# Decoder block on one core: the first batch of x in four transfers, its moments and transposes tile by tile, 14 warming products for 26

## The chip, the core and the metric

The kernel runs on one core of a Trainium2 chip. A core has a matrix engine (TensorE, here PE, with its weight loads listed apart as PEld), a vector engine (VectorE, DVE), a scalar engine (ScalarE, ACT), a general engine (GpSimd, POOL), a queue-only engine (SyncE, SP) and 16 DMA engines that move data between HBM and SBUF. Each engine runs its own stream of instructions in program order; the streams meet only in semaphores that one engine raises and another waits on. Matrix products read SBUF and write PSUM banks; DVE and ACT read PSUM and write SBUF. The metric is the device time of one execution in microseconds.

## The reference

```python
x = x + attn(layernorm(x), q_weight, v_weight, out_w, out_b)     # x is (4, 512, 256)
x = x + xattn(layernorm(x), ctx, ...)                            # 16 heads of 64, 64 keys a batch
x = x + ffn(layernorm(x), Ws, bs, W1, b1, W2, b2)                # 8 experts, each takes its top 256 rows

def attn(x, q_weight, v_weight, out_w, out_b):                   # attention over the first axis, of length 4
    q = einsum('tbm,mhd->tbhd', x, q_weight)
    q_sq = einsum('tbhd,tbhd->tbh', q, q)
    squared_dist = q_sq[:, None] + q_sq[None, :] - 2.0 * einsum('tbhd,sbhd->tsbh', q, q)
    attn_weights = softmax(-squared_dist / sqrt(head_dim), axis=1)
    A = einsum('mhd,nhd->hmn', q_weight, q_weight) / sqrt(head_dim)
    PXA = einsum('tsbh,sbhm->tbhm', attn_weights, einsum('tbm,hmn->tbhn', x, A))
    return einsum('tbhm,mhd->tbhd', PXA, v_weight).reshape(...) @ out_w.T + out_b
```

All of it is computed in float32. Only the first few microseconds of the first line matter for this change.

## The kernel before, in words

The program is written as one stream per engine (`sp_part1`, `act_part1`, `dve_part1`, `pool_part1`, `pe_part1`, and parts 2 to 4 behind them). Nothing is reordered by a planner: what stands in a function is the order on that engine, and the only thing that makes an engine wait is a semaphore.

x has 4 x 512 rows of 256, held in SBUF as `X`, 16 tiles of 128 rows; tile `t * NJ + j` holds rows 128j to 128j + 127 of position t. The first attention mixes the four positions t of one row, so part 1 works in four blocks j of T = 4 tiles each. "The first batch" is block j = 0.

The way of block 0 to the first use of its queries, with the semaphores in brackets:

- SP starts all loads, in the order x block 0, `wqa` (the query weight), x block 1, ctx, two more weights, x blocks 2 and 3, and then the four 1 MB weights Wq, Wk, Wv, Wo. The load of one x block is one transfer of 512 KB [`ld_x[j]`].
- DVE, `statistics(0)`: four BN_STATS (one a tile), then four BN_AGGR, which give mean and variance of each row [`var1_ready`].
- POOL, `inverse_std`: adds eps, raises to -0.5 [`powers`, after two of its four operations], then multiplies the mean by it and negates it [`rstd1_ready`].
- The four normalised tiles `xn1` are made by two engines: tiles 1 to 3 by DVE (line 673, behind `powers`), tile 0 by ACT (`normalise(0, (0,))`, behind `rstd1_ready`). Each raises `xn1_ready` by one.
- PE, `xn_transpose(0)`: eight 128 x 128 transposes (four tiles, two column halves m) into banks 0 and 1, behind `xn1_ready` = 4.
- ACT, `xnT_evac(0)`: copies both banks to `xnT` [`xnT_ready`].
- PE, `q_product(0)`: eight float32 products of 128 x 256 [`full`], after four transposes of ctx.
- ACT copies the queries to `q` [`q_ready`], and DVE's `differences(0)` (lines 643 to 645) forms the differences of the positions' queries. From there the chain goes on to squares (ACT), distances and weights (DVE), and so through the block.

Ahead of its first transpose PE runs `WARM_UP` = 26 products of the identity with itself, whose result nothing reads. They wait for the identity alone.

DVE's order around this matters for the prediction: `statistics(0)`, the three normalised tiles, `statistics(1)`, `statistics(2)`, `statistics(3)`, each behind its block's load, and only then `differences(0)`. So does the order on PE: warming, transposes of block 0, ctx transposes (behind the load of ctx), `q_product(0)`.

Of the kernel before, what the change touches and what calls it, by code (L numbers as in the profile page):

```python
# [13 lines left out]
def build_program(nc, A, out):  # L14
# [108 lines left out]
    with ctx:  # L123
# [6 lines left out]
        def overlay(*sets):  # L130
# [96 lines left out]

        ld_x = [sem(f"ld_x{j}") for j in range(NJ)]
        ld = {n: sem(f"ld_{n}") for n in ("cols", "ctx", "wqa", "attw", "outb", "small", "ws", "wq", "wk", "wv")}
        xn3_stored = sem("xn3_stored")  # L230
# [11 lines left out]
        H_hi_ready, H_ready = sem("H_hi_ready"), sem("H_ready")  # L242
        var1_ready, rstd1_ready, xn1_ready, xnT_ready, q_ready = (
            sem(n) for n in ("var1_ready", "rstd1_ready", "xn1_ready", "xnT_ready", "q_ready"))
        dif_ready, sq_ready, dist_ready, ex_ready, weighted, summed, scaled, mixed, mixT_ready = (
# [88 lines left out]
        def sp_part1(sp):  # L334
            def load_x(j):
                sp.dma_start(X[:, j::NJ, :], x_rows[:, j::NJ, :]).then_inc(ld_x[j], 16)

            load_x(0)
            sp.dma_start(wqa[:], wq_s).then_inc(ld["wqa"], 16)
            load_x(1)  # L340
            sp.dma_start(ctx_sb, ctx_rows).then_inc(ld["ctx"], 16)
            sp.dma_start(owa, ow_s).then_inc(ld["attw"], 16)
            sp.dma_start(wva, wv_s).then_inc(ld["attw"], 16)
            load_x(2)
            load_x(3)
            sp.dma_start(Wq[:], chunked(A["L0_xattn_Wq"])).then_inc(ld["wq"], 16)
            sp.dma_start(Wk[:], chunked(A["L0_xattn_Wk"])).then_inc(ld["wk"], 16)
            sp.dma_start(Wv[:], chunked(A["L0_xattn_Wv"])).then_inc(ld["wv"], 16)
            sp.dma_start(Wo[:], chunked(A["L0_xattn_Wo"])).then_inc(xn3_stored, 16)
# [47 lines left out]
        def pool_part1(pool, order):  # L397
# [19 lines left out]
            for s in range(NJ):  # L417
                if s >= 1:
                    pool.wait_ge(scaled, s)
                    g.tensor_tensor(acc[:], acc[:], q[:, (s - 1) % 2], ALU.add).then_inc(mixed, 1)  # L420
                pool.wait_ge(xn1_ready, T * (s + 1))
                g.tensor_tensor(X[:, s::NJ, :], X[:, s::NJ, :],
                                outb_bc[:].unsqueeze(1).to_broadcast([P, T, D]), ALU.add).then_inc(xb_ready, 1)
# [19 lines left out]
        def act_part1(act):  # L443
            a = nc.scalar
            def normalise(j, tiles=range(T)):
# [3 lines left out]
                for t in tiles:  # L449
                    i = t * NJ + j  # L450
                    a.activation(xn1[:, t], X[:, i], ACT.Identity, bias=nmean[:, i:i + 1],
                                 scale=rstd[:, i:i + 1]).then_inc(xn1_ready, 1)

# [66 lines left out]
            act.dma_start(bs_bc[:], row_broadcast(A["L0_ffn_bs"], E)).then_inc(ld["small"], 16)  # L520
            act.wait_ge(ld_x[0], 16)
            xnT_evac(0)
# [64 lines left out]
        def dve_part1(dve, order):  # L587
            v = nc.vector

            def statistics(j, var_ready):  # L590
                for t in range(T):
                    ins = v.bn_stats(stats[:, t * NJ + j, :], X[:, t * NJ + j, :])
                order(ins)
# [73 lines left out]

            dve.wait_ge(ld_x[0], 16)
            statistics(0, var1_ready)
            dve.wait_ge(powers, 1)  # L670
            for t in range(1, T):
                i = t * NJ
                v.tensor_scalar(xn1[:, t], X[:, i], mv[:, i, 0:1], rstd[:, i:i + 1], ALU.subtract,
                                ALU.mult).then_inc(xn1_ready, 1)
            for j in range(1, NJ):
# [51 lines left out]

        WARM_UP = 26

        def pe_part1(pe):  # L730
            t = nc.tensor

            def xn_transpose(j):
# [67 lines left out]
            for _ in range(WARM_UP):  # L801
                t.matmul(banks[7][:, 0:P], ident[:], ident[:], start=True, stop=True)  # L802
            xn_transpose(0)
            pe.wait_ge(ld["ctx"], 16)
# [1197 lines left out]
```

## Time and profile before

| | |
|---|---|
| runs | 354.67, 352.87, 354.94 us; median 354.67 us |
| profiled execution | 353.8 us, its span in the trace 351.9 us, mean granted TensorE clock 0.952 |
| PE busy | 312.6 us (89% of the span) |
| DVE busy | 289.1 us (82%) |
| POOL busy | 198.7 us (56%) |
| ACT busy | 188.6 us (54%) |
| moved by DMA | 34.26 MB |

The profile is of one execution. Times in it count from the start of the span. A row of the timeline or of the chain of waits begins with its start and its length in us; the chain of waits is the work that ended last, followed back from the end of the kernel, so that an operation in it delayed what followed. A float32 product on PE stands in the trace as two records.

### The profile page before, as it was taken

What the parts mean: (1) busy time and instruction counts of PE and PEld (TensorE: products, weight loads), DVE (VectorE), ACT (ScalarE), POOL (GpSimd) and SP (SyncE); (2) the same over time, 40 slices, a digit from 0 to 9 for tenths busy, and PEclk for the clock granted to TensorE, in tenths of its full rate; (3) what the DMA queues carried; (4) which work ended last, traced back from release to release, by engine and by line L of the source; (5) the groups of instructions that cost most, each with busy time, mean ns of one, the idle gap of its engine ahead of it and who ended that gap; (6) DMA issues with size and microseconds to landing.
All of it is one profiled execution on the core that took longest, in us unless ns stands there. A gap on an engine that the chain in (4) does not pass through costs nothing.

```text
span 351.9 us, 6208 instructions
## 1 busy us (share of the span) xinstructions
PE 312.6 (89%) x2200; PEld 277.3 (79%) x2200; DVE 289.1 (82%) x664; ACT 188.6 (54%) x374; POOL 198.7 (56%) x256
## 2 busy tenths in 40 slices
PE   7988999998789999999999992129999999999991
PEld 7877787776579999999999891128999998899990
DVE  2789899979988988788887877778798997999960
ACT  1576765448536565667655645790426736742230
POOL 3768898853234458877888765703264623643232
PEclk9999999999999999999999995556999999999998
DMA  8970000000000406225042437301367957621222
GB/s 244 378 251 1 3 0 2 0 2 1 0 2 15 136 16 210 71 81 182 30 149 77 134 106 241 119 1 32 95 200 191 262 154 207 151 28 32 32 30 30
DMA packets 24045, 34.26 MB, mean 97 GB/s; under 512 B 1784, under 2 KB 20560, under 8 KB 23888
## 3 DMA queue, kind: packets, MB, share of 16 engines
q1 hardware_dynamic: 20112, 29.36, 25.6%
q0 software_dynamic: 3072, 4.20, 7.0%
q10 hardware_dynamic: 832, 0.32, 0.4%
q8 instruction: 17, 0.28, 0.3%
q14 instruction: 12, 0.10, 0.1%
HBM read 27.58 MB, written 6.29 MB: 96 GB/s over the span
## 4 chain that ended last, share of the span: by engine, by line
PE 65%; DVE 19%; POOL 6%; issue 3%; DMA 3%; ACT 2%; POOLq 0%; DVEq 0%; ACTq 0%
PE bank L970 9%; PE bank L972 8%; PE bank L971 8%; PE bank L1742 5%; PE bank L1010 4%; PE q_banks L970 4%; PE q_banks L972 3%; PE q_banks L971 3%; PE bank L802 3%; PE bank L1743 2%; DVE flags_all L1485 2%; DMA out_x<-ybuf,idx 2%; PE q_banks L747 2%; PE bank L765 2%; PE bank L781 2%
## 5 line engine op out<-in xcount | busy, mean ns | idle before, releaser
L1816 POOL DMA_INDIRECT out_x<-ybuf,idx x16 | 26.2, 1637 | 46.9 <-DVE ybuf L1840 44.7
L1742 PE MATMUL bank<-W,h_hi 128*128 128x512 f32 x112 | 41.0, 407 | 0.2
L970 PE MATMUL bank<-H,PT_hi 128*128 128x256 f32 x128 | 36.5, 285 | 0.4 <-DVE PT_lo L1293 0.3
L1161 ACT ACTIVATE prob<-prob 128x1024 f32<-128x1024 f32 x16 | 17.0, 1060 | 36.2 <-DVE prob L1335 36.2
L972 PE MATMUL bank<-H,PT_lo 128*128 128x256 f32 x128 | 36.2, 283 | 0.0
L971 PE MATMUL bank<-H,PT_hi 128*128 128x256 f32 x128 | 36.2, 283 | 0.0
L1201 POOL TENSOR_TENSOR prob<-prob,rsum 128x1024 f32<-128x1024 f32 x15 | 28.6, 1906 | 12.1 <-DVE rsum L1310 12.1
L1795 POOL DMA_INDIRECT xg<-xn_rows,idx x16 | 20.6, 1285 | 26.0 <-DVE idx L1873 22.0
L1772 ACT ACTIVATE hbuf<-bank,b_cols 128x256 f32<-128x256 f32 x32 | 13.5, 472 | 37.1 <-PE bank L972 37.1
L1743 PE MATMUL bank<-W,h_lo 128*128 128x256 f32 x112 | 31.4, 280 | 0.0
L970 PEld LDWEIGHTS bank<-H,PT_hi 128*128 128x128 f32 x128 | 24.5, 191 | 1.5 <-issue 0.9
L1742 PEld LDWEIGHTS bank<-W,h_hi 128*128 128x128 f32 x112 | 21.1, 188 | 5.6 <-DVE h_lo L1929 1.2
L971 PEld LDWEIGHTS bank<-H,PT_hi 128*128 128x128 f32 x128 | 24.5, 191 | 0.5
L972 PEld LDWEIGHTS bank<-H,PT_lo 128*128 128x128 f32 x128 | 24.5, 191 | 0.0
L1929 DVE TENSOR_TENSOR h_lo<-hbuf,h_hi 128x512 fp32r<-128x512 f32 x32 | 22.2, 693 | 1.1
L1743 PEld LDWEIGHTS bank<-W,h_lo 128*128 128x128 f32 x112 | 21.2, 189 | 0.0
L1293 DVE TENSOR_TENSOR PT_lo<-bank,PT_hi 128x512 fp32r<-128x512 f32 x32 | 20.0, 666 | 1.1 <-ACT PT_hi L1125 1.1
L1304 DVE TENSOR_REDUCE sums<-prob 128x16 f32<-128x1024 f32 x15 | 18.3, 1220 | 2.8 <-ACT prob L1161 2.4
L1772 ACT ACTIVATE hbuf<-q_banks,b_cols 128x256 f32<-128x256 f32 x32 | 13.4, 471 | 11.9 <-PE q_banks L972 6.0
L1010 PE MATMUL bank<-ident,prob 128*128 128x128 f32 x128 | 17.1, 276 | 2.8 <-DVE H L947 2.8
L1927 DVE CAST h_hi<-hbuf 128x512 fp32r<-128x512 f32 x32 | 14.2, 445 | 5.6 <-ACT hbuf L1772 5.6
L1186 POOL TENSOR_TENSOR rstd<-mv,eps_col 128x1 f32<-128x1 f32 x16 | 3.1, 192 | 27.9 <-DVE mv L1312 24.9
(298 smaller groups left out, 1088.6 us busy)
## 6 DMA issues: line engine op xcount, KB each, us to landing
W_raw<-in_L_ffn_W SPq DMA_DIRECT2D x8, 1024.0 KB, 5.6
W_in<-in_L_ffn_W SPq DMA_DIRECT2D x8, 1024.0 KB, 6.5
X<-in_x SPq DMA_DIRECT2D x4, 512.0 KB, 6.4
xn_rows<-xn SPq DMA_DIRECT2D x16, 128.0 KB, 1.7
out_x<-X SPq DMA_DIRECT2D x4, 512.0 KB, 3.6
Wq<-in_L_xattn_Wq SPq DMA_DIRECT2D x1, 1024.0 KB, 11.0
Wk<-in_L_xattn_Wk SPq DMA_DIRECT2D x1, 1024.0 KB, 12.3
Wv<-in_L_xattn_Wv SPq DMA_DIRECT2D x1, 1024.0 KB, 15.1
```

The lines of the kernel that those rows point to most:

```text
L970: t.matmul(out_ps, hi, rhs_hi, start=first, stop=False)
L971: t.matmul(out_ps, hi, rhs_lo, start=False, stop=False)
L972: return t.matmul(out_ps, lo, rhs_hi, start=False, stop=last_one)
L1010: mm = t.transpose(banks[4 + g][:, c * P:(c + 1) * P], flat[:, o:o + P], ident[:])
L1201: g.tensor_tensor(prob[:, s], prob[:, s], rsum[:, s].unsqueeze(2).to_broadcast([P, HX, CK]), ALU.mult).then_inc(prob_ready, 1)
L1293: nc.vector.tensor_tensor(PT_lo[:, n % 2, c], v3(banks[4 + g][:], 4), raw(PT_hi[:, n % 2, c]), ALU.subtract).then_inc(PT_ready, 1)
L1742: t.matmul(v3(banks[6 + h][:], 2), h_hi[:, f, hs], W2[:, f, :, p], start=f == 0, stop=False)
L1743: mm = t.matmul(banks[6 + h][:, 0:D], h_lo[:, f, hs], W2_hi[:, p, f], start=False, stop=f == FC - 1)
L1772: ins = a.activation(hbuf[:, g % 2, f % 2], banks[g][:, (f % 2) * CAP:(f % 2 + 1) * CAP], ACT.Gelu_apprx_tanh, bias=b1_cols[:, e * FC + f: ...
L1795: g.indirect_dma_start(xg[:, s, h], None, xn3_dram, bass.IndirectOffsetOnAxis(ap=idx[:, e, h:h + 1], axis=0), bounds_check=last_row, oob_i ...
L1816: g.indirect_dma_start(out_flat, bass.IndirectOffsetOnAxis(ap=idx[:, e, h:h + 1], axis=0), ybuf[:, h], None, bounds_check=last_row, oob_is ...
L1929: v.tensor_tensor(h_lo[:, fs], hbuf[:, g_ % 2], raw(h_hi[:, fs]), ALU.subtract).then_inc(h_ready, 1)
```

## The change

- The load of x block 0 becomes four transfers of 128 KB, one a tile, each with a semaphore of its own (`ld_x0[t]`). They stand where the one transfer stood, first on SP. Blocks 1 to 3 are loaded as before.
- DVE's `statistics(0)` waits for each tile just ahead of that tile's BN_STATS; the wait for the whole block in front of it is gone.
- DVE's three normalised tiles now raise `first_xn1_ready`, one each. ACT's tile 0 raises `xn1_ready` by T = 4 at once, so that all later counts of `xn1_ready` stay as they were. POOL, which writes over X block 0 later (line 422), waits for both.
- PE's eight transposes of block 0 (`first_xn_transposes`) go tile by tile, in the order 1, 2, 3, 0, each pair behind its own tile. Before, all eight waited for all four tiles, and went bank by bank.
- `WARM_UP` is 14.

```diff
@@ sp_part1
-            load_x(0)
+            for t in range(T):
+                sp.dma_start(X[:, t * NJ, :], x_rows[:, t * NJ, :]).then_inc(ld_x0[t], 16)
             sp.dma_start(wqa[:], wq_s).then_inc(ld["wqa"], 16)
@@ pool_part1
                 pool.wait_ge(xn1_ready, T * (s + 1))
+                if s == 0:
+                    pool.wait_ge(first_xn1_ready, T - 1)
@@ act_part1, normalise
                     a.activation(xn1[:, t], X[:, i], ACT.Identity, bias=nmean[:, i:i + 1],
-                                 scale=rstd[:, i:i + 1]).then_inc(xn1_ready, 1)
+                                 scale=rstd[:, i:i + 1]).then_inc(xn1_ready, T if j == 0 else 1)
@@ act_part1
-            act.wait_ge(ld_x[0], 16)
+            for t in range(T):
+                act.wait_ge(ld_x0[t], 16)
             xnT_evac(0)
@@ dve_part1, statistics
                 for t in range(T):
+                    if j == 0 and var_ready is var1_ready:
+                        dve.wait_ge(ld_x0[t], 16)
                     ins = v.bn_stats(stats[:, t * NJ + j, :], X[:, t * NJ + j, :])
@@ dve_part1
-            dve.wait_ge(ld_x[0], 16)
             statistics(0, var1_ready)
             dve.wait_ge(powers, 1)
             for t in range(1, T):
                 i = t * NJ
                 v.tensor_scalar(xn1[:, t], X[:, i], mv[:, i, 0:1], rstd[:, i:i + 1], ALU.subtract,
-                                ALU.mult).then_inc(xn1_ready, 1)
+                                ALU.mult).then_inc(first_xn1_ready, 1)
@@ pe_part1
-        WARM_UP = 26
+        WARM_UP = 14
...
+            def first_xn_transposes():
+
+                ps = [bank_free(f"T0{m}") for m in range(MC)]
+                for r in (*range(1, T), 0):
+                    pe.wait_ge(*((first_xn1_ready, r) if r else (xn1_ready, T)))
+                    for m in range(MC):
+                        mm = t.transpose(ps[m][:, r * P:(r + 1) * P], xn1[:, r, m * P:(m + 1) * P], ident[:])
+                        if r == 0:
+                            filled(mm, f"T0{m}")
...
-            xn_transpose(0)
+            first_xn_transposes()
             pe.wait_ge(ld["ctx"], 16)
```

On PE, from its first product to the first query product, the stream before reads as follows (line, operation, output and inputs, and in brackets what it waits for; `xn` is xn1, `dif` at line 809 the buffer in which ctx lies):

```order
L802 MATMUL bank<-ident 128x128 [waits ident_ready]
L802 MATMUL bank<-ident 128x128 x25
L738 MATMUL bank<-ident,xn 128x128 [waits xn1_ready]
L738 MATMUL bank<-ident,xn 128x128 x7
L809 MATMUL bank<-ident,dif 128x128 [waits ld_ctx]
L809 MATMUL bank<-ident,dif 128x128 x3
L747 MATMUL q_banks<-wqa,xnT 128x256 [waits xnT_ready,ld_wqa]
```

and now:

```order
L818 MATMUL bank<-ident 128x128 [waits ident_ready]
L818 MATMUL bank<-ident 128x128 x13
L745 MATMUL bank<-ident,xn 128x128 [waits first_xn1_ready]
L745 MATMUL bank<-ident,xn 128x128
...
L745 MATMUL bank<-ident,xn 128x128 [waits xn1_ready]
L745 MATMUL bank<-ident,xn 128x128
L825 MATMUL bank<-ident,dif 128x128 [waits ld_ctx]
L825 MATMUL bank<-ident,dif 128x128 x3
L763 MATMUL q_banks<-wqa,xnT 128x256 [waits xnT_ready,ld_wqa]
```

Twelve warming products are gone, one wait became four, and what comes behind the transposes kept its place.

On SP, the loads of part 1 before:

```order
L336 DMA X<-in_x 128x4x256
L339 DMA wqa<-in_L_attn_q_weight 128x2x256
L336 DMA X<-in_x 128x4x256
L341 DMA dif<-in_ctx 128x2x256
L342 DMA dif<-in_L_attn_out_w 128x2x256
L343 DMA dif<-in_L_attn_v_weight 128x2x256
L336 DMA X<-in_x 128x4x256 x2
```

and now:

```order
L340 DMA X<-in_x 128x256 x4
L341 DMA wqa<-in_L_attn_q_weight 128x2x256
L337 DMA X<-in_x 128x4x256
L343 DMA dif<-in_ctx 128x2x256
L344 DMA dif<-in_L_attn_out_w 128x2x256
L345 DMA dif<-in_L_attn_v_weight 128x2x256
L337 DMA X<-in_x 128x4x256 x2
```

Every later load, x block 2 among them (the first of the pair in the last row), now stands three issues further back.

On DVE, from the first moments to the moments of block 2 before:

```order
L592 BN_STATS stats<-X 128x6 [waits ld_x0]
L592 BN_STATS stats<-X 128x6 x3
L595 BN_AGGR mv<-stats 128x2 [waits dve_order]
L595 BN_AGGR mv<-stats 128x2 x3
L673 TENSOR_SCALAR xn<-X,mv,rstd 128x256 [waits powers]
L673 TENSOR_SCALAR xn<-X,mv,rstd 128x256 x2
L592 BN_STATS stats<-X 128x6 [waits ld_x1]
...
L592 BN_STATS stats<-X 128x6 [waits ld_x2]
```

and now:

```order
L599 BN_STATS stats<-X 128x6 [waits ld_x0_0]
L599 BN_STATS stats<-X 128x6 [waits ld_x0_1]
L599 BN_STATS stats<-X 128x6 [waits ld_x0_2]
L599 BN_STATS stats<-X 128x6 [waits ld_x0_3]
L602 BN_AGGR mv<-stats 128x2 [waits dve_order]
L602 BN_AGGR mv<-stats 128x2 x3
L679 TENSOR_SCALAR xn<-X,mv,rstd 128x256 [waits powers]
L679 TENSOR_SCALAR xn<-X,mv,rstd 128x256 x2
L599 BN_STATS stats<-X 128x6 [waits ld_x1]
...
L599 BN_STATS stats<-X 128x6 [waits ld_x2]
```

The order of the work is the same; the one wait in front of the four BN_STATS is now one wait ahead of each, and the wait for x block 2 is where it was.

## Rows read from the trace of the kernel before

**Rows 1.** Chain of waits, first 17 us: start, length, engine, tile, line.

```profile
1.83 8.86 PE bank L802 x52
10.69 0.45 PE bank L738 x4
11.23 1.09 ACT xnT L457 x2
12.46 3.71 PE q_banks L747 x16
16.19 0.61 ACT q L464
```

**Rows 2.** Timeline of DVE to 17 us; in brackets idle time before, and its releaser.

```profile
4.83 1.41 DVE L592 BATCH_NORM_STATS2 stats<-X 128x6 f32<-128x256 f32 x4 [4.83 <-DMA X<-in_x]
6.27 0.38 DVE L595 BATCH_NORM_AGGREGATE mv<-stats 128x2 f32<-128x6 f32 x4
8.19 1.32 DVE L673 TENSOR_SCALAR xn<-X,mv,rstd 128x256 f32<-128x256 f32 x3 [1.54 <-POOL rstd L406]
...
10.85 0.38 DVE L595 BATCH_NORM_AGGREGATE mv<-stats 128x2 f32<-128x6 f32 x4
11.58 1.41 DVE L592 BATCH_NORM_STATS2 stats<-X 128x6 f32<-128x256 f32 x4 [0.35 <-DMA X<-in_x]
...
13.31 1.37 DVE L592 BATCH_NORM_STATS2 stats<-X 128x6 f32<-128x256 f32 x4
...
16.82 0.96 DVE L643 TENSOR_TENSOR dif<-q_banks,q 128x768 f32<-128x768 f32 x1 [1.72 <-ACT q L464]
```

**Rows 3.** Warming products still to come from two times on: ns min/median/max, first and last start.

```profile
L802 PE MATMUL bank<-ident x46: 274/275/421, 3.3 to 10.4; 128*128 128x128 f32 x46 
...
L802 PE MATMUL bank<-ident x25: 274/275/275, 7.7 to 10.4; 128*128 128x128 f32 x25 
```

**Rows 4.** Window: PE, PEld, DVE, ACT, POOL busy, granted clock, DMA share, GB/s.

```profile
3.00:4.00 1.00, 1.00 (x7) 1.00 (x6) 0.00 (x0) 0.00 (x0) 0.00 (x0) 1.00 1.04 348
```

**Rows 5.** Timeline of the SP queue; last, all issues of 128 KB stores (ns).

```profile
0.79 0.42 SPq L336 DMA_DIRECT2D X<-in_x  x1
...
1.82 0.46 SPq L336 DMA_DIRECT2D X<-in_x  x1
2.32 0.51 SPq L341 DMA_DIRECT2D dif<-in_ctx  x1
...
3.92 1.06 SPq L336 DMA_DIRECT2D X<-in_x  x2
...
7.69 0.71 SPq L348 DMA_DIRECT2D Wv<-in_L_xattn_Wv  x1
...
L1407 SPq DMA_DIRECT2D xn_rows<-xn x16: 319/332/343, 110.4 to 218.3; - x16
```

**Rows 6.** Issue to landing in us: x blocks 0, 1, ctx, x block 2, Wv; last, later stores.

```profile
X<-in_x SPq DMA_DIRECT2D x1, 512.0 KB, 4.0
...
X<-in_x SPq DMA_DIRECT2D x1, 512.0 KB, 5.2
dif<-in_ctx SPq DMA_DIRECT2D x1, 256.0 KB, 5.8
...
X<-in_x SPq DMA_DIRECT2D x1, 512.0 KB, 7.6
...
Wv<-in_L_xattn_Wv SPq DMA_DIRECT2D x1, 1024.0 KB, 15.1
...
xn_rows<-xn SPq DMA_DIRECT2D x16, 128.0 KB, 1.7
```

**Rows 7.** Timeline of ACT, PE and POOL further on.

```profile
8.82 0.60 ACT L451 ACTIVATE xn<-X,nmean,rstd 128x256 f32<-128x256 f32 x1 [6.53 <-POOL nmean L408]
...
26.10 1.28 POOL L438 TENSOR_TENSOR acc<-dif 128x512 f32<-128x512 f32 x1 [2.18 <-DVE dif L664]
...
27.99 1.03 PE L781 MATMUL bank<-ctxT,Wv 128*128 128x256 f32 x4
```

More of the change, by code:

```diff
@@ L228, in build_program @@
         ld_x = [sem(f"ld_x{j}") for j in range(NJ)]
+        ld_x0 = [sem(f"ld_x0_{t}") for t in range(T)]
         ld = {n: sem(f"ld_{n}") for n in ("cols", "ctx", "wqa", "attw", "outb", "small", "ws", "wq", "wk", "wv")}
@@ L242, in build_program @@
         H_hi_ready, H_ready = sem("H_hi_ready"), sem("H_ready")
-        var1_ready, rstd1_ready, xn1_ready, xnT_ready, q_ready = (
-            sem(n) for n in ("var1_ready", "rstd1_ready", "xn1_ready", "xnT_ready", "q_ready"))
+        var1_ready, rstd1_ready, xn1_ready, first_xn1_ready, xnT_ready, q_ready = (
+            sem(n) for n in ("var1_ready", "rstd1_ready", "xn1_ready", "first_xn1_ready", "xnT_ready", "q_ready"))
         dif_ready, sq_ready, dist_ready, ex_ready, weighted, summed, scaled, mixed, mixT_ready = (
```

## The prediction

> **What bounds the kernel now.** I read the chain of waits first, for what stands in the first microseconds, since every edit lies there. It shows PE alone from 1.83 us on: the 26 warming products, then the transposes, then the copy on ACT, the query products, the copy of the queries, and behind them DVE's differences [rows 1, 2]. The reader is to see that the chain's first 9 us are products whose result nobody reads. The four normalised tiles were ready earlier: DVE's three at 8.19 + 1.32 = 9.51 us [rows 2], ACT's one at 8.82 + 0.60 = 9.42 us [rows 7]. The last warming record starts at 10.4 us and lasts 0.275 us [rows 3]. So the transposes waited about a microsecond for the warming, and below that, hidden by it, lies the chain load, moments, POOL, normalised tiles.
>
> Next the DVE timeline, for what comes when both get shorter. DVE goes from block 0's tiles to the moments of blocks 1, 2 and 3, and only then to `differences(0)`. It already waits in there, 0.35 us for x block 2 until 11.58 us, and it ends at 16.82 - 1.72 = 15.10 us, 1.72 us ahead of the queries [rows 2]. Those 1.72 us are the room for every gain at the start: past them DVE, and through it the load of x block 2, sets the time. The landings confirm it: block 2 was issued at 3.92 us and took 7.6 us, so it landed at 11.52 us [rows 5, 6].
>
> **The change part by part.**
>
> *The moments.* The 512 KB landed at 0.79 + 4.0 = 4.79 us [rows 5, 6], and then came four BN_STATS in 1.41 us and four BN_AGGR, to 6.65 us [rows 2]. With a tile each, three of the BN_STATS run while later tiles land, and only the last stands behind the last landing: 1.41 / 4 = 0.35 us in place of 1.41, a gain of 1.06 us if the last tile lands at 4.79 us as the block did. No row shows a load split so. The bounds: the last tile could land earlier or later by what the issue moves. The fourth issue starts later by three issues, 3 x 0.33 to 3 x 0.42 us, 1.0 to 1.3 us (the 128 KB stores' issue, and that of the whole block [rows 5]). Of that little should reach the landing: from 3 us on the DMA engines are busy without a break, at 348 GB/s [rows 4], and the 512 KB need 1.5 us at that rate, so the fourth tile's bytes come last either way. I take 4.8 us, and keep 4.5 to 5.4. So `var1_ready` comes at 5.6 instead of 6.65 us.
>
> *The normalised tiles.* POOL's way is the same work: DVE starts 1.54 us after the moments, ACT 2.17 us after [rows 2, 7]. Tiles 1 to 3 then run from 7.14 to 8.46 us, the first done at 7.6; ACT's tile is ready at 8.37 us. Signalling tile by tile costs nothing that a row shows, since each of these instructions raised a semaphore before too.
>
> *The warming products.* 46 of the 52 records were left at 3.3 us and 25 at 7.7 us, so 21 records took 4.4 us, 0.21 us each; the last 24 steps took 2.7 us, 0.11 us each [rows 3]. That is the lower and the upper of the clock's two levels (1.2 and 2.4 GHz) by the spacing, though the column of the granted clock reads 1.00 from 3 to 4 us, in the slow stretch [rows 4]; I go by the spacing. PE had run products without a break since 1.83 us when the rate doubled, about 7.5 us. Fourteen products are 28 records; the 28th started at 7.7 us and ended at about 8.0 us. So 12 products, 2.7 us, are gone, and the end of the warming now falls at 8.0 us, 0.4 us behind the first tile and ahead of the last. The warming no longer decides.
>
> *The transposes.* Tiles 1 and 2 follow the warming at once, tile 3 at 8.46 us, tile 0 at about 8.7 us: four records of 0.11 us behind the last tile, and the first full bank at about 8.95 us. Before, four transposes ended at 11.14 us and ACT began at 11.23 us [rows 1]; now it begins near 9.0 us. Both banks are filled by the last pair, so ACT can no longer copy bank 0 while bank 1 is filled; that costs about two records, 0.2 us, and is in the sum. ACT's copies take 1.09 us and the first query product begins at 12.46 - 11.23 = 1.23 us behind them [rows 1], at 10.2 us. The ctx transposes ahead of it need ctx, which landed at 2.32 + 5.8 = 8.1 us [rows 5, 6] and now between that and 9.4 us (by the 1.3 us above); their four records fit before 10.2 us either way. The query products end at 13.9 us, ACT's last copy at 14.5 us, against 16.80 [rows 1]. This branch gains 2.3 us.
>
> *What is late next.* DVE ends block 0's tiles at 8.46 us and block 1's moments 1.72 us later (9.51 to 11.23 us before [rows 2]), at 10.2 us; block 1 landed at 7.02 us [rows 5, 6], and even 1.3 us later it is there. Then DVE waits for x block 2. Its bytes stand behind all that SP issued before it, and the engines are saturated, so a later issue should be made good in the queue: between 0 and 1.3 us of delay, and I take 0.2, near zero, since the row nearest to it is the DMA share above 1.0 [rows 4]. From 11.52 + 0.2 = 11.7 us, two blocks of moments (11.58 to 15.10 us before, 3.52 us [rows 2]) end at 15.25 us. The queries are there at 14.5 us. So `differences(0)` starts at 15.3 instead of 16.82 us: a gain of **1.5 us**, of 2.3 that PE's branch offers.
>
> *Behind that* I see nothing that gives it back. POOL, busy with tables until then, waits 2.18 us for DVE's weighted differences at 26.10 us [rows 7]; its own work moves up by about 1 us with the moments. The last load that part 1 waits for, Wv, landed at 7.69 + 15.1 = 22.8 us and is first used beside Wk at 27 us [rows 5 to 7]; 1.5 us earlier on one side and up to 1.3 later on the other still leave room. From there on every wait is on another engine, so the shift goes through to the end.
>
> *The sum.* The profiled execution took 353.8 us, 0.9 under the median of the three runs, 354.67. These four times average 354.07 us, and I set the sum on that: 354.07 - 1.5 = **352.6 us**.
>
> **The rivals.**
>
> *The queue delay reaches x block 2.* All 1.0 to 1.3 us of the three issues arrive, DVE's moments end at 16.2 to 16.4 us, and the gain is 0.4 to 0.6 us: 353.6 us. For it: DVE waited there already. Against it: engines that never run dry.
>
> *The whole of PE's branch counts.* If block 2 lands 0.8 us earlier, as its issue gets ahead of the small loads of ACT's queue or because the transfers settle faster, 2.3 us arrive: 351.8 us. Against it: nothing in the change brings it forward.
>
> *The query products run at the lower clock* (slower). The rate doubled at record 26 or 27, and the change keeps 28. If in an execution it doubles later, or the pauses between the four pairs put it off, the query products, 3.71 us [rows 1], take 7.4: from 10.2 to 17.6 us, the copy to 18.2 us, and `differences(0)` starts 1.4 us later than before, 355.5 us. It decides once the products are slow for more than about 2.3 of their 3.71 us. Against it: while the clock is low the transposes too take twice as long and fill PE's pauses. The Trainium skill, "TensorE: Matmul & The Clock Gate", Part 1, says that how many products run slowly at the start differs from run to run of one kernel and should not be fitted to a count; by it, a fixed 14 is a margin of one product here that another execution may not have. One trace cannot show the spread.
>
> *The transfers land one after the other* (slower). A 128 KB transfer on a quieter queue takes 1.7 us from issue to landing [rows 6]. If each of the four had to land before the next moves on, the last tile would come at 0.79 + 4 x 1.7 = 7.6 us, 2.8 us later than the block did, and x block 2 behind it at 14.3 us; two blocks of moments then end at 17.9 us, and `differences(0)` starts 1.0 us later than before: 355.1 us. It decides once block 2 lands over 1.7 us late. Against it: x block 1 landed 2.2 us and ctx 3.3 us after block 0 although each took over 5 us from its issue [rows 5, 6], so transfers of one queue overlap. The Trainium skill, "DMA: Bandwidth & Descriptors", Anatomy of one DMA, gives a fixed cost of some 2 us to each transfer and its rules advise large ones; paid in series, three more would cost 6 us, and the landings just named disagree with that.
>
> **How the numbers follow.** The forecast has 0.62, the queue delay 0.15, the whole branch 0.10, the lower clock 0.08, the serial landing 0.05. Predicted is 352.6 us. The range goes from 351.2 (the fastest run, 352.87, less the whole room of 1.7) to 355.0 us, which leaves out most of the lower clock and a little of the noise, since the four times of one kernel spread over 2.1 us. A change of 1% (3.5 us), about what a measurement of this kernel can tell from none, is more than any branch gives: faster by over 1% has 0.05 (the whole branch with a lucky median), slower by over 1% 0.03 (the lower clock for longer than the query products), within 1% 0.92.
>
> **What would show it.** In the profile after, the warming ends near 8 us or earlier; block 0's BN_STATS are spread between 4 and 5.2 us; DVE's moments end near 5.6 us; `xnT` begins near 9 us and the query products near 10.2 us, in 3.7 us; DVE waits more than 1 us for x block 2, and `differences(0)` follows the moments of block 3 without a wait, near 15.3 us. A DVE wait for ACT's `q` there would say that PE's branch decides after all; query products of over 5 us, the clock; a later part of the chain that starts at the old times, that something behind took the gain back.

## The result and the profile after

The changed kernel took 356.81 us (median of 9 runs, 356.07 to 360.00), the kernel before 354.03 us (9 runs, 352.53 to 354.94), timed in turn: a ratio of **1.0095** (95% interval 1.0071 to 1.0118). It is slower by 2.8 us where 352.6 us was predicted, outside the range and in the other direction. The profiled execution of after is its slowest, 360.0 us with a span of 358.0. Runs over 1.5% above the fastest of their kernel are left out of the ratios but not of the medians, so the two can differ, and the profile of outb_late below is of such a run and is not read.

The chain of waits of after (start, length, engine, tile, line) no longer begins with the warming:

```profile
5.51 9.16 DMA X<-in_x
14.70 1.42 DVE stats L599 x4
16.52 1.38 DVE stats L599 x4
20.11 1.48 ACT sq L474
21.59 0.98 ACT xnT L461 x2
22.62 5.42 PE q_banks L763 x16
...
61.23 1.09 PE bank L772 x8
```

It starts with one load, x block 2. The DVE timeline of after, in answer to [rows 2]:

```profile
2.98 0.43 DVE L599 BATCH_NORM_STATS2 stats<-X 128x6 f32<-128x256 f32 x1 [2.98 <-DMA X<-in_x]
3.63 0.86 DVE L599 BATCH_NORM_STATS2 stats<-X 128x6 f32<-128x256 f32 x2 [0.22 <-DMA X<-in_x]
5.53 0.43 DVE L599 BATCH_NORM_STATS2 stats<-X 128x6 f32<-128x256 f32 x1 [1.04 <-DMA X<-in_x]
...
14.70 1.41 DVE L599 BATCH_NORM_STATS2 stats<-X 128x6 f32<-128x256 f32 x4 [3.76 <-DMA X<-in_x]
...
18.22 0.93 DVE L650 TENSOR_TENSOR dif<-q_banks,q 128x768 f32<-128x768 f32 x1
```

The tiles' moments are spread over their landings, as foreseen, and DVE waits 3.76 us for x block 2, with no wait between block 3's moments and `differences(0)`, as foreseen too. But block 2 comes at 14.70 us, not at 11.7, against 11.58 before. Of those 3.12 us of delay the 1.72 us that DVE used to wait for the queries [rows 2] take up part; the rest, 1.40 us, is how much later `differences(0)` starts.

The SP queue of after, in answer to [rows 5]:

```profile
0.79 1.81 SPq L340 DMA_DIRECT2D X<-in_x  x4
2.65 0.43 SPq L341 DMA_DIRECT2D wqa<-in_L_attn_q_weight  x1
3.12 0.55 SPq L337 DMA_DIRECT2D X<-in_x  x1
3.71 0.73 SPq L343 DMA_DIRECT2D dif<-in_ctx  x1
...
5.51 2.73 SPq L337 DMA_DIRECT2D X<-in_x  x2
```

Four issues take 1.81 us, so everything behind them up to x block 2 is issued 1.3 to 1.6 us later than before (ctx 2.32 before, x block 2 3.92). The issues of x blocks 2 and 3 together, 1.06 us before [rows 5], now take 2.73 us. In the ACT queue of after, whose issues stand where they stood before:

```profile
3.67 0.60 ACTq L520 DMA_DIRECT2D ws_sb<-in_L_ffn_Ws  x1
4.30 0.48 ACTq L521 DMA_DIRECT2D outb_bc<-in_L_attn_out_b  x1
```

Those are the loads of `Ws` and of `out_b` (one row, read for all 128 partitions). Before, x block 2 and all that stands ahead of it on SP were issued by 3.92 us or begun then [rows 5], ahead of `out_b`. Now ctx goes out level with `Ws`, and owa, wva (the two more weights, out_w and v_weight) and x block 2 behind `out_b`. How full the DMA engines are meanwhile (PE, PEld, DVE, ACT, POOL, granted clock, DMA share, GB/s), before:

```profile
4.00:5.00 1.00, 1.00 (x7) 1.00 (x7) 0.17 (x1) 0.00 (x0) 0.00 (x0) 1.00 1.09 380
8.00:9.00 1.00, 1.00 (x12) 1.00 (x11) 0.81 (x2) 0.18 (x1) 0.76 (x4) 1.00 1.19 322
```

and after:

```profile
4.00:5.00 1.00, 1.00 (x7) 1.00 (x7) 0.48 (x2) 0.00 (x0) 0.00 (x0) 1.00 0.61 187
8.00:9.00 1.00, 0.59 (x3) 0.36 (x4) 1.00 (x3) 0.41 (x1) 0.83 (x4) 1.00 0.48 94
...
23.00:24.00 1.00, 1.00 (x4) 0.79 (x3) 1.00 (x3) 0.51 (x3) 0.59 (x1) 0.56 1.04 348
24.00:25.00 1.00, 1.00 (x4) 0.78 (x3) 0.93 (x7) 1.00 (x3) 0.00 (x0) 0.50 0.87 280
```

The DMA share has two holes. From 4 to 5 us the engines move 187 GB/s, where they moved 380. From 8 to 9 us they are half idle at 94 GB/s, although ctx, owa, wva and x block 2 have been issued, 1.25 MB, and none of these loads is complete (the first lands at 11.3 us). The last two rows show a second loss: PE's clock at 0.50, the lower level. PE's timeline, before and then after:

```profile
21.25 3.72 PE L747 MATMUL q_banks<-wqa,xnT 128*128 128x256 f32 x16 [0.94 <-ACT xnT L457]
```

```profile
1.83 5.39 PE L818 MATMUL bank<-ident 128*128 128x128 f32 x28 [1.83 <-POOL ident L361]
8.37 1.55 PE L745 MATMUL bank<-ident,xn 128*128 128x128 f32 x8 [1.15 <-DVE xn L679]
11.70 0.66 PE L825 MATMUL bank<-ident,dif 128*128 128x128 f32 x4 [1.77 <-DMA dif<-in_ctx]
12.19 3.62 PE L763 MATMUL q_banks<-wqa,xnT 128*128 128x256 f32 x16
...
22.62 5.41 PE L763 MATMUL q_banks<-wqa,xnT 128*128 128x256 f32 x16 [2.65 <-ACT xnT L461]
```

The query products of block 1 start 1.37 us later and last 1.69 us longer. They stand behind `differences(0)`: ACT copies block 1's `xnT` after the squares of `differences(0)`, as the chain shows. PE has all its other work done by 20.0 us, waits 2.65 us where it waited 0.94, and then runs at the lower level for most of the 5.41 us.

So 1.40 + 1.69 = 3.1 us are lost by 28 us. A product of eight records that the chains of both kernels hold is 2.90 us late, at 61.23 us against 58.33 (that row of before stands in the last experiment). The span of this execution lost 6.1 us (358.0 against 351.9), the median 2.8. Another 1.0 of the 6.1 is a fall of the clock near 100 us, treated below, and the last 2.2 lie behind 241 us, where the clock fell once more. That window of after (before reads 1.00 in it):

```profile
246.00:260.00 14.00, 12.71 (x96) 12.13 (x97) 8.30 (x20) 4.51 (x11) 2.80 (x2) 0.76 0.14 32
```

### The profile page after: what moved, and what is told of

It reads as the page before. It is cut to its first block, busy times and chain, and to the rows that moved or that the text cites. A ratio compares the mean times of both kernels' runs of the same rounds, so it can differ in the third digit from the quotient of the medians.

```text
span 358.0 us, 6165 instructions
## 1 busy us (share of the span) xinstructions
PE 314.1 (88%) x2176; PEld 278.0 (78%) x2176; DVE 289.9 (81%) x664; ACT 189.0 (53%) x374; POOL 197.9 (55%) x256
## 4 chain that ended last, share of the span: by engine, by line
PE 67%; DVE 16%; POOL 6%; DMA 3%; issue 3%; ACT 2%; SPq 1%; DVEq 0%; POOLq 0%
PE bank L986 9%; PE bank L988 9%; PE bank L987 9%; PE bank L1758 6%; PE bank L1026 4%; PE q_banks L986 4%; PE q_banks L988 4%; PE q_banks L987 4%; PE bank L1759 3%; DMA X<-in_x 3%; PE q_banks L763 3%; DVE flags_all L1501 2%; PE bank L781 2%; PE bank L797 2%; POOL acc L422 1%
## 5 line engine op out<-in xcount | busy, mean ns | idle before, releaser
L1788 ACT ACTIVATE hbuf<-q_banks,b_cols 128x256 f32<-128x256 f32 x32 | 13.4, 471 | 11.6 <-PE q_banks L988 6.2
L986 PE MATMUL bank<-xgT_hi,W_hi 128*128 128x256 f32 x64 | 19.3, 302 | 0.0
```

The lines of the kernel that those rows point to most:

```text
L986: t.matmul(out_ps, hi, rhs_hi, start=first, stop=False)
L1788: ins = a.activation(hbuf[:, g % 2, f % 2], banks[g][:, (f % 2) * CAP:(f % 2 + 1) * CAP], ACT.Gelu_apprx_tanh, bias=b1_cols[:, e * FC + f: ...
```

## The experiments

Each kernel was timed in five rounds against the kernel before on the same chip (medians of before there 353.56 to 353.86 us). Where the positions of a profile matter they are in this table, in us, from one profile a kernel: when DVE begins x block 2's moments (as a rule its landing), when `differences(0)` starts, start and length of block 1's query products. One profile is one draw: after, after_again, after_filled and split_only have the same loads, and their block 2 comes between 13.08 and 14.70 us; outb_on_sp and outb_on_sp_filled have the same loads too, and it comes at 12.66 and 11.80. With SP's loads as in before it spreads less (11.58, 11.60, 11.70).

| kernel | median | ratio (95% interval) | block 2 | differences(0) | query products, block 1 |
|---|---|---|---|---|---|
| before | 354.03 | | 11.58 | 16.82 | 21.25, 3.72 |
| after | 356.81 | 1.0095 (1.0071 to 1.0118) | 14.70 | 18.22 | 22.62, 5.41 |
| after_again | 356.67 | 1.0088 (1.0048 to 1.0127) | 13.95 | 17.61 | 22.01, 5.36 |
| split_only | 357.44 | 1.0085 (1.0050 to 1.0120) | 13.08 | 17.26 | 21.66, 5.41 |
| warm14_only | 353.86 | 1.0014 (0.9986 to 1.0043) | 11.70 | 17.11 | 21.54, 3.72 |
| one_load | 353.11 | 0.9986 (0.9955 to 1.0017) | 11.60 | 15.69 | 20.12, 3.72 |
| issue_delay | 356.24 | 1.0066 (1.0044 to 1.0089) | 13.63 | 17.64 | 22.04, 5.41 |
| after_filled | 355.03 | 1.0013 (0.9984 to 1.0041) | 14.59 | 18.16 | 23.36, 3.62 |
| after_act_late | 357.32 | 1.0042 (1.0007 to 1.0078) | 11.46 | 15.10 | 21.27, 4.72 |
| two_queues | 355.94 | 1.0050 (1.0024 to 1.0077) | 13.29 | 17.06 | 21.46, 5.26 |
| before_act_early | 354.84 | 1.0014 (0.9977 to 1.0050) | 12.59 | 16.19 | 20.62, 3.72 |
| outb_late | 355.66 | 1.0030 (1.0000 to 1.0061) | not read | not read | not read |
| outb_late_x2_first | 355.31 | 1.0030 (0.9996 to 1.0064) | 11.08 | 17.41 | 21.80, 6.50 |
| outb_on_sp | 355.66 | 1.0053 (1.0026 to 1.0080) | 12.66 | 16.96 | 21.36, 6.25 |
| outb_on_sp_x2_first | 355.48 | 1.0055 (1.0026 to 1.0083) | 10.69 | 15.84 | 20.24, 5.28 |
| outb_on_sp_filled | 354.69 | 1.0032 (1.0003 to 1.0062) | 11.80 | 15.92 | 20.54, 3.62 |

### Which part of the change

**after_again** is the changed kernel once more, beside the three that follow.

> The changed kernel once more, for a second trace of it. If the late landing of x block 2 (14.67 us in the first trace, 11.52 before) belongs to the four transfers, it lands between 13.5 and 15 us again, differences(0) starts between 17.5 and 18.7 us, and the time is 1.0085 to 1.010 of before. If the first trace, the slowest of its runs, only caught an accident of the DMA engines, block 2 lands near 12 us here and the loss must lie elsewhere.

It repeated the result, in positions too.

**split_only**: before, with the four transfers and DVE's waits tile by tile, 26 warming products and the old transposes.

```diff
-            load_x(0)
+            for t in range(T):
+                sp.dma_start(X[:, t * NJ, :], x_rows[:, t * NJ, :]).then_inc(ld_x0[t], 16)
...
+                    if j == 0 and var_ready is var1_ready:
+                        dve.wait_ge(ld_x0[t], 16)
```

> Four transfers and moments tile by tile, but 26 warming products and the transposes as before. Theory of the loads: x block 2 lands near 14.5 us, differences(0) starts near 18 us, the time is 1 to 2.5 us over before. Theory of the clock (14 warming products let the clock fall later, in the second query products): nothing is lost here, 353.5 to 354.5 us, and the second query products take 3.7 us.

It loses as much as the whole change within the intervals, with the same two signs: block 2 late at 13.08 us, block 1's query products 5.41 us long.

**warm14_only**: before, with `WARM_UP = 14`.

> The kernel before with 14 warming products and nothing else. Theory of the loads: the transposes start at 9.6 us, x block 2 lands at 11.5 us as before, and the time is 0.7 to 1.0 us under before (353.0 to 353.4). Theory of the clock: the query products or those of block 1 run at the lower level for part of their time, 355.5 to 357 us.

No difference that can be measured, neither the gain nor the loss of the two theories. PE waits 2.01 us ahead of the transposes, and the query products of block 0 take 4.66 us instead of 3.69: here, and only here, the lower clock falls into block 0.

**one_load**: after, with block 0 loaded by one transfer.

```diff
-            for t in range(T):
-                sp.dma_start(X[:, t * NJ, :], x_rows[:, t * NJ, :]).then_inc(ld_x0[t], 16)
+            load_x(0)
```

> The changed kernel with block 0 in one transfer again: transposes tile by tile and 14 warming products stay. Theory of the loads: x block 2 lands at 11.5 us, differences(0) starts at 15.3 to 15.9 us, 352.6 to 353.4 us. Theory of the clock: as the changed kernel, 355.5 to 357 us.

`differences(0)` starts 1.13 us earlier than before, and the loss is gone. So the four transfers are what costs; the rest of the change, without them, brings the start forward, and still the median is only 0.7 us lower, with 1 inside the interval. Where the gain goes, and how much of the 1.13 us is one, is in the last part.

### Why the four transfers cost: their size, or the issues behind them

**issue_delay**: before, its one load of block 0 kept whole, with four small loads (4 KB each, read by nobody) on SP right behind it.

```diff
             load_x(0)
+            for k in range(4):
+                sp.dma_start(shifted_key[8 * k:8 * k + 8, :],
+                             A["L0_xattn_bq"].rearrange("(c p) -> c p", p=P)).then_inc(ld_extra, 16)
```

> The kernel before, block 0 in one transfer, with four small loads (4 KB each, into a buffer that nothing reads before it is written anew) behind it on SP, so that every later load is issued about 1.4 us later, as in the changed kernel, and nothing is split. If the later issue alone does the harm, x block 2 lands at 12.8 to 14.7 us, differences(0) starts at 16.8 to 18 us and the time is 0.4 to 1.0% over before. If it is the splitting into small transfers, block 2 lands at 11.5 to 12.2 us and the time is that of before within 0.3%.

Nothing is split, and it loses in the same way, as its first branch had it. Its DVE timeline, windows and PE row (columns as above):

```profile
13.63 1.41 DVE L597 BATCH_NORM_STATS2 stats<-X 128x6 f32<-128x256 f32 x4 [2.54 <-DMA X<-in_x]
15.90 1.41 DVE L597 BATCH_NORM_STATS2 stats<-X 128x6 f32<-128x256 f32 x4 [0.46 <-DMA X<-in_x]
```

```profile
4.00:5.00 1.00, 1.00 (x7) 1.00 (x7) 0.31 (x1) 0.00 (x0) 0.00 (x0) 1.00 0.61 158
8.00:9.00 1.00, 1.00 (x11) 1.00 (x11) 0.95 (x3) 0.32 (x1) 0.75 (x5) 1.00 0.71 117
```

```profile
22.04 5.41 PE L752 MATMUL q_banks<-wqa,xnT 128*128 128x256 f32 x16 [2.78 <-ACT xnT L461]
```

Block 2 is 2.05 us late and the same two holes stand in the DMA share. So the first block need not come in four parts for the loss: it is enough that SP's later loads are issued 1.4 to 1.6 us later, behind four more transfers. Whether those four small transfers do harm of their own, beside the lateness, this run can't tell.

**after_act_late**: after, with ACT's loads of `b1`, `Ws` and `out_b` issued behind its copy of block 0's `xnT`.

```diff
-            act.dma_start(b1_raw[:], A["L0_ffn_b1"].rearrange("e (c p) -> (e c) p", p=P)).then_inc(ld["cols"], 16)
-            act.dma_start(ws_sb[:], chunked(A["L0_ffn_Ws"])).then_inc(ld["ws"], 16)
-            act.dma_start(outb_bc[:], row_broadcast(A["L0_attn_out_b"], D)).then_inc(ld["outb"], 16)
             normalise(0, (0,))
...
             xnT_evac(0)
+            act.dma_start(b1_raw[:], A["L0_ffn_b1"].rearrange("e (c p) -> (e c) p", p=P)).then_inc(ld["cols"], 16)
+            act.dma_start(ws_sb[:], chunked(A["L0_ffn_Ws"])).then_inc(ld["ws"], 16)
+            act.dma_start(outb_bc[:], row_broadcast(A["L0_attn_out_b"], D)).then_inc(ld["outb"], 16)
```

> The changed kernel with three of ACT's loads (b1, Ws, out_b) issued behind block 0's copies instead of at 3 to 4.8 us. If x block 2 is late because these loads now stand level with SP's and are served ahead of it, it lands 0.7 to 1.5 us earlier than in the changed kernel (12.3 to 13.3 us for 13.9 to 14.7) and the time falls by 1 us or more, to 354 to 355.8. If the gaps in the queue's own supply do it, block 2 moves by less than 0.5 us and the time by less than 0.5.

SP issues nearly as late as in after (x block 2 at 5.21 us, 5.51 in after), and yet block 2 is there at 11.46 us, ahead of the forecast too, and the second hole is gone:

```profile
11.46 1.40 DVE L599 BATCH_NORM_STATS2 stats<-X 128x6 f32<-128x256 f32 x4 [1.58 <-DMA X<-in_x]
...
15.10 0.93 DVE L650 TENSOR_TENSOR dif<-q_banks,q 128x768 f32<-128x768 f32 x1
```

```profile
4.00:5.00 1.00, 1.00 (x7) 1.00 (x7) 0.90 (x3) 0.00 (x0) 0.00 (x0) 1.00 0.81 188
...
8.00:9.00 1.00, 1.00 (x9) 0.79 (x8) 1.00 (x4) 0.26 (x2) 0.36 (x2) 1.00 1.05 341
```

The first hole stays (188 GB/s from 4 to 5 us, 187 in after), so the late issue by itself, without ACT's three loads, costs block 2 nothing here; what costs goes with the second hole. With ACT's loads out of the way `differences(0)` starts at 15.10 us, as forecast for the change (15.3). The Trainium skill, "DMA: Bandwidth & Descriptors", section "Issuing engines are not separate DMA queues", says that transfers issued by different engines run on the same 16 DMA engines and interleave; this pair of runs agrees, since moving three loads on ACT's queue moved a load on SP's queue by 3.2 us. That the engines are shared does not by itself explain the delay, for in after they stood half idle meanwhile. By the ratio half of the loss is gone (1.0042 for 1.0095, the intervals just overlap), by the median none (357.32 us), and the kernel is no faster than before: `Ws` itself now lands too late for PE, which works in order:

```profile
19.77 0.76 PE L848 MATMUL bank<-ws_sb,mean_of 128*128 128x8 f32 x4 [2.27 <-DMA ws_sb<-in_L_ffn_Ws]
...
21.27 4.72 PE L763 MATMUL q_banks<-wqa,xnT 128*128 128x256 f32 x16
```

**two_queues**: after, with tiles 2 and 3 issued by ACT, first on its queue (the added lines), so that SP issues only two.

```diff
-            for t in range(T):
+            for t in range(2):
                 sp.dma_start(X[:, t * NJ, :], x_rows[:, t * NJ, :]).then_inc(ld_x0[t], 16)
...
+            for t in range(2, T):
+                act.dma_start(X[:, t * NJ, :], x_rows[:, t * NJ, :]).then_inc(ld_x0[t], 16)
```

> The changed kernel with tiles 2 and 3 of block 0 issued by ACT ahead of its table load, tiles 0 and 1 by SP: SP is set back by one issue (0.45 us) instead of three. If the set-back of SP's later loads is the cause, x block 2 lands at 11.5 to 12.5 us, differences(0) starts near 15.3 to 16 us, and the time is 352.3 to 353.5. If transfers of 128 KB as such do it, block 2 is as late as in the changed kernel (13.9 us or later) and the time 356 to 357.

SP issues x block 2 at 4.63 us, half as late as in after; block 2 lands at 13.29 us, between the two forecasts, and the loss is about half (1.0050).

**before_act_early**: before, with the same three ACT loads issued first on ACT (0.80 to 2.02 us) and SP untouched.

> The kernel before, its SP stream untouched, with ACT's loads of b1, Ws and out_b issued ahead of its table load, so that they stand in front of most of SP's loads without SP being late. If standing behind these three loads is what costs, x block 2 lands at 12.3 to 13.5 us, differences(0) starts at 16.8 to 17.3 us and the time is 0 to 0.7% over before. If only a late SP does harm, block 2 lands at 11.5 to 11.9 us and nothing changes.

Block 2 is 1.0 us late (12.59 us) with SP's issues up to it at most 0.2 us later than before (4.08 against 3.92 us). That a load of ACT's which gets ahead delays block 2 is shown here without a change on SP; the whole 3.1 us isn't, nor a loss of time (1.0014, with 1 inside the interval). `differences(0)` came at 16.19 us, ahead of the forecast and of the 16.82 of before: the warming took 8.18 us in this execution and 8.86 in that of before, and the queries came 0.63 us earlier.

**outb_late** (after; `out_b` behind ACT's normalised tile, `bo` and `bs` behind `xnT`), **outb_on_sp** (after; `out_b` on SP behind x block 3), and each with x block 2 ahead of owa and wva (**_x2_first**). The edit of outb_on_sp:

```diff
             load_x(3)
+            sp.dma_start(outb_bc[:], row_broadcast(A["L0_attn_out_b"], D)).then_inc(ld["outb"], 16)
...
-            act.dma_start(outb_bc[:], row_broadcast(A["L0_attn_out_b"], D)).then_inc(ld["outb"], 16)
```

> The changed kernel with ACT's load of out_b alone (128 KB, one row read 128 times) issued behind its normalised tile instead of at 4.3 us; b1 and Ws stay early, so that nothing waits for them. If out_b, served ahead of SP's later loads, is what holds x block 2 back, block 2 lands at 11.5 to 12.3 us, differences(0) starts at 15.1 to 15.8 us, block 1's query products take 3.7 us, and the time is 352.0 to 353.5. If the small pieces of Ws and b1 are as much to blame, block 2 lands at 12.5 us or later and half the loss stays (355 to 356).

> As outb_late, with x block 2 issued on SP ahead of two weights of 256 KB. Block 2 lands at 10 to 11 us, DVE ends its moments near 14 us, and PE's branch decides (queries at 14.3 to 14.6 us): differences(0) starts at 14.5 to 15 us, 351 to 352.5 us. If the start no longer sets the time, it is that of outb_late.

> The changed kernel with the load of out_b moved from ACT's queue to SP's, behind x block 3 and ahead of Wq, so that it cannot stand in front of or level with any load of x. If out_b's place is the cause, x block 2 lands at 11.5 to 12.2 us and block 3 by 13.8 us, differences(0) starts at 15.2 to 15.8 us, block 1's query products take 3.7 us, and the time is 352.3 to 353.5, the gain that was forecast. If the gaps of SP's late issue are the cause, block 2 lands at 12.5 us or later and the time is 355 or more.

> As outb_on_sp, with x block 2 issued ahead of two weights. If block 2 sets the time, it lands near 10.5 us and differences(0) starts at 14.5 to 15.3 us, 351.5 to 353 us; if block 3 does, differences(0) starts no earlier than in outb_on_sp and the time is the same.

With `out_b` moved, block 2 comes at 12.66 us in outb_on_sp, by its expectation the branch in which the gaps of SP's issue are to blame, and at 11.80 in outb_on_sp_filled (below), whose loads are the same, in the branch of `out_b`. Put further forward on SP it comes at 11.08 us (outb_late_x2_first) and 10.69 (outb_on_sp_x2_first), and then block 3 is the late one (its moments start at 15.67 and 14.11 us, 13.31 before). The second hole goes with `out_b`: from 8 to 9 us the DMA engines move 327 GB/s in outb_on_sp and 373 in outb_on_sp_filled, and a shallower dip comes from 12 to 14 us (231 and 249 GB/s, 250 and 219). So `out_b` has a large part in the delay. The late issue without ACT's loads cost block 2 nothing (after_act_late); how much `Ws` and `b1` add stays open. In the three of these four whose profile is read, block 1's query products run at the lower clock for part of the way (5.28 to 6.50 us), and none of the four is faster than before, where 351 to 353.5 us was expected.

### The clock in block 1's query products

**after_filled**: after, with ten idle products (into a free bank) on PE right ahead of block 1's query products, where it waits.

```diff
             WqT_transpose(0)
+            pe.wait_ge(ctxT_ready, 1)
+            for _ in range(10):
+                t.matmul(banks[4][:, 0:P], ident[:], ident[:], start=True, stop=True)
             q_product(1)
```

> The changed kernel with ten more products of the identity with itself, whose result nothing reads, ahead of block 1's query products, where PE idled 2.5 us. If the fall of the clock in those query products (5.4 us for 3.7 before) is the second half of the loss, they take 3.7 us here and the time falls by 1.3 to 1.9 us against the changed kernel, to 354.8 to 355.5. If the late loads alone set the time, it stays at 356.4 to 357.

PE's timeline and windows:

```profile
19.60 3.93 PE L854 MATMUL bank<-ident 128*128 128x128 f32 x20
23.36 3.62 PE L763 MATMUL q_banks<-wqa,xnT 128*128 128x256 f32 x16
```

```profile
18.00:19.00 1.00, 0.35 (x4) 0.26 (x3) 1.00 (x5) 0.00 (x0) 0.83 (x3) 1.00 1.00 401
19.00:20.00 1.00, 0.99 (x6) 0.99 (x7) 1.00 (x4) 0.00 (x0) 0.84 (x2) 0.69 1.03 414
20.00:21.00 1.00, 1.00 (x7) 1.00 (x6) 0.35 (x2) 0.95 (x1) 0.83 (x3) 0.50 1.01 402
...
23.00:24.00 1.00, 1.00 (x8) 0.94 (x7) 1.00 (x3) 0.56 (x3) 0.39 (x1) 1.00 1.11 348
```

Block 2 is as late as in after (14.59 us), and the time falls: by 1.8 us by the medians, by 0.8% by the ratios. So the clock is a loss of its own beside the late load. Its size is better read from the positions: the query products start 0.74 us later and end 1.05 us sooner, and the product of the chain near 60 us comes at 60.16 us, 1.07 sooner than in after. The rest of the 1.8 us may lie further on, since this profile lacks the fall of the clock near 100 us (last part). The filling did not hold the clock up: it fell at 19.4 us, behind a wait of 0.66 us for Wq and ahead of the first idle product (19.60 us); the idle products ran through the slow stretch in place of the query products.

**outb_on_sp_filled** joins both remedies.

> As outb_on_sp, with ten more products of the identity with itself, whose result nothing reads, ahead of block 1's query products. If PE's idle time there still lets the clock fall, they take 3.7 us here and over 4.5 us in outb_on_sp, and this is 1 us faster; if the clock holds without them, the ten products cost 0 to 1 us.

Block 1's query products start at 20.54 us, 0.71 us before those of before, and take 3.62 us, and the median is 1.0 us under that of outb_on_sp (6.25 us there), both as expected, though the intervals of the ratios overlap. The granted clock stays at 1.00 from 15 to 26 us. That the idle products held it is not shown: PE had waited only 0.25 us for Wq ahead of them, 1.35 us in outb_on_sp. The median is 1.1 us over before all the same, and no row here says why; the profiled execution, 353.49 us, is 1.2 us under it.

### Where a gain at the start goes

The chain of waits of before and of one_load, at two products far apart:

```profile
58.33 1.09 PE bank L756 x8
237.36 1.17 PE bank L1681 x16
```

```profile
57.17 1.09 PE bank L768 x8
237.09 1.17 PE bank L1693 x16
```

one_load is 1.16 us ahead at 57 us, all of its start's gain, and 0.27 us ahead at 237. From one product to the other it takes 179.92 us, before 179.03. The windows that differ, of one_load and then of before (columns as above):

```profile
95.00:100.00 5.00, 3.48 (x14) 3.22 (x15) 3.84 (x7) 2.40 (x5) 1.38 (x2) 0.68 0.00 0
```

```profile
95.00:100.00 5.00, 2.27 (x15) 2.09 (x16) 3.87 (x8) 2.24 (x4) 2.57 (x2) 1.00 0.00 0
```

This stretch is the same code in all kernels. In the profiles of one_load, warm14_only, after, after_again, split_only, issue_delay, two_queues, after_act_late, outb_on_sp_x2_first and outb_on_sp_filled the granted clock falls somewhere from 95 to 105 us, and the way between these two products takes 179.88 to 180.12 us; in before, before_act_early, after_filled, outb_late_x2_first and outb_on_sp it doesn't fall there, and the way takes 178.83 to 179.08 us. So the fall costs about 0.9 us, most of the 1.16 by which one_load leads. Whether it comes is not set by being early or late: of the kernels that reach the first product ahead of before, one_load and outb_on_sp_filled have it and before_act_early (57.67 us) hasn't. One profile a kernel can't tell whether the kernel sets it or the execution.

Nor is the lead of one_load all the kernel's doing. issue_delay computes block 0 as before does, with 26 warming products and the old transposes:

```profile
1.83 7.62 PE L807 MATMUL bank<-ident 128*128 128x128 f32 x52 [1.83 <-POOL ident L363]
...
11.41 3.69 PE L752 MATMUL q_banks<-wqa,xnT 128*128 128x256 f32 x16 [0.46 <-ACT xnT L461]
```

and one_load:

```profile
11.33 3.69 PE L759 MATMUL q_banks<-wqa,xnT 128*128 128x256 f32 x16 [0.78 <-ACT xnT L459]
```

The 52 warming records took 8.86 us in the profile of before [rows 1], and 7.62, 7.69 and 8.18 us in issue_delay, split_only and before_act_early. With the 7.62 us the query products of block 0 start at 11.41 us, not at 12.46, within 0.08 us of one_load. So the profile of before was a late one at the start, and in an execution like that of issue_delay most of one_load's 1.13 us would not be there to gain.

## Why the prediction was wrong

- **The step that failed**: "the engines are saturated, so a later issue should be made good in the queue: between 0 and 1.3 us of delay, and I take 0.2". It measured 3.1 us in after, and 1.5 to 2.4 in split_only, issue_delay and after_again; the later issue alone was 1.3 to 1.6 us, at 0.45 us an issue, where 1.0 to 1.3 was reckoned. I took the DMA share of one microsecond before [rows 4] as a property that a later issue leaves alone. issue_delay shows that the share itself depends on it (1.09 becomes 0.61 at 4 to 5 us, 1.19 becomes 0.71 at 8 to 9), and after_act_late that what ACT's queue has issued by then decides, since with its three loads out of the way block 2 came at 11.46 us: I had set SP's later loads against SP's own queue alone, and not against ACT's.
- **The second step that failed**: "Behind that I see nothing that gives it back". A DVE that is late leaves PE idle ahead of block 1's query products (2.65 us for 0.94), and they run at the lower level for most of their time: 1.69 us more, of which after_filled gives back 1.05. That the idle time brings the fall was not tested by itself and goes by comparing the profiles: where PE waits 0.94 us there (before, warm14_only, one_load, before_act_early) the clock stays up, and in every kernel whose wait there is longer it is down, though in after_again it had fallen ahead of that wait. The rival of the lower clock had the mechanism, but in block 0, where it happened only in warm14_only, with 4.66 us.
- In after's profile the two make 4.6 us: `differences(0)` at 18.22 instead of 15.3 us is 2.9, the clock 1.7. That 352.6 + 4.6 = 357.2 comes near the median of 356.81 is in part luck, since that profile is of the slowest execution. In after_again, an execution of 356.84 us, they make 2.3 + 1.6 = 3.9, and the fall near 100 us adds 0.9, to 357.4.
- **A term sized on one execution**: the 1.72 us of room, and with it the gain of 1.5, came from a profile whose warming was the longest of four with 26 products. In issue_delay the same work has the queries at 15.74 us in place of 16.80; against the 15.10 us at which before's moments end, the room would have been 0.6 us. Even with block 2 on time the forecast gain was too large for such an execution.
- **The rivals**: "the queue delay reaches x block 2" had the right place with a bound of 1.3 us. "The transfers land one after the other" came nearest in numbers (block 2 at 14.3, `differences(0)` 1.0 us late, decisive over 1.7 us), but its mechanism is not what happened: DVE has the four tiles by 2.98 to 5.53 us, at a median of 2.3 us from issue to landing, not 1.7 us one after the other, and issue_delay does the same without them. The fixed cost of some 2 us that the prediction takes there from the Trainium skill, "DMA: Bandwidth & Descriptors", Anatomy of one DMA, is measured in that section on transfers that GpSimd issues; SP issues these.
- **The last tile** landed at 5.53 us, not at 4.8, over the bound of 5.4; in outb_late_x2_first, with the same four transfers, DVE waited for it until 4.65 us. It did not decide, since DVE waited later anyway.
- **Right**: the warming ended at 7.2 us ("near 8 us or earlier"), ahead of the first normalised tile, and no longer decides. DVE's wait for x block 2 sets the time, with `differences(0)` behind it at once. The query products of block 0 came at 12.19 us, not 10.2: half of that comes with the late last tile (ACT's copies of `xnT` begin at 10.01 us, not 9.0), half with ctx, which landed 2.2 us behind the bound given (11.6 us against 9.4). With both in time they came at 10.11 us, and `differences(0)` at 15.10 (after_act_late), as forecast.
- The Trainium skill, "TensorE: Matmul & The Clock Gate", Part 1, was cited for a count of slow products that varies between executions. That agrees: the 28 warming records took 4.74 us in one_load, 5.39 in after and 6.27 in outb_on_sp_filled.

## What to carry to other kernels

Splitting a transfer is paid by what its queue issues next, and by what other queues get ahead meanwhile: list the loads of all queues by time of issue, before and after, ahead of trusting a full DMA share. Where an engine's wait grows, look at who idles behind it: PE's next products may run at the lower clock, which here cost as much again (1.69 us beside 1.40). A gain of a microsecond at the start is worth what is left at the end; compare two products far apart in both chains. And before counting on a microsecond of room, see whether it stands in a second profile of the same kernel.

## What was not expected of the hardware

- 1.4 us of later issue made a 512 KB load land 1.5 to 3.1 us later, while the DMA engines stood half idle (0.48 of their time, 94 GB/s) with over 1 MB issued and not landed. With ACT's three small loads elsewhere the same engines moved 341 GB/s in that microsecond, with `out_b` alone elsewhere 327. Why so few bytes hold so much up isn't shown.
- What PE did before the granted clock fell differs. In after it had stood idle from 20.0 to 22.6 us, and the clock fell at 23.1, in the products behind. In after_filled it fell at 19.4 us, with PE at 0.35 of its time from 18 to 19 us, and in after_again at 18.5 us, behind waits of PE of 0.34 and 0.54 us and ahead of the long one (2.45 us). An idle stretch of 0.94 us in before was followed by no fall. What decides it isn't shown.
